# Channel stage: sums' products behind a convolution, attention-out seven ahead, first and last operations shared out differently

## What is computed

```
x = x + attn(cond(x, itok), ...)                    # ends in: o @ Wo.T + bo
# second block, along time (T = 512), per channel and batch
mask = arange(T) < length[batch]
y = causal_conv(x * mask, kernel[channel])          # 512 taps, from 64 complex modes
y = (y + x * mask * D[channel]) * mask
w = (q6 - zero_point) * scale                       # 512 x 512
x = x + y @ w.T + bias
```

## Time and profile before

| | |
|---|---|
| median of 3 runs | 736.43 us (736.04 to 737.22) |
| the profiled execution's own time | 739.18 us |
| its span, first to last instruction | 737.3 us |
| PE busy in the span | 707.4 us (96%) |
| DVE, ACT, POOL busy | 589.8, 412.7, 205.9 us (80%, 56%, 28%) |
| last stage, 572.5 us to the end | 164.8 us |

### The profile page before, as it was taken

The page is one execution under the profiler, slowest core; times in us unless marked ns, Lnnn a source line. Parts: engine busy times, 40 slices in busy tenths (PEclk is TensorE's granted clock), DMA queues, the critical chain, the costliest instruction groups (busy, mean ns, idle before and its releaser), DMA issues.

```text
span 737.3 us, 17037 instructions
## 1 busy us (share of the span) xinstructions
PE 707.4 (96%) x7152; PEld 568.3 (77%) x7152; DVE 589.8 (80%) x1010; ACT 412.7 (56%) x736; POOL 205.9 (28%) x237
## 2 busy tenths in 40 slices
PE   8999999999999999999999999999989799999997
PEld 7767787786978788787869787887667687777785
DVE  5778989998997877697767868777987688788754
ACT  5576565655656765846555565648554444444433
POOL 5361020030002010540300000006200176766676
PEclk9999999999999999999999999999999999999999
DMA  7800100010002001000100010012112678888732
GB/s 224 316 3 2 58 5 1 2 62 2 2 1 63 2 2 58 2 4 13 61 2 2 1 59 2 1 32 74 44 63 49 180 196 207 196 210 182 181 99 101
DMA packets 31919, 50.94 MB, mean 69 GB/s; under 512 B 6594, under 2 KB 21090, under 8 KB 30562
## 3 DMA queue, kind: packets, MB, share of 16 engines
q1 hardware_dynamic: 29858, 49.26, 24.4%
q0 software_dynamic: 1024, 0.53, 0.3%
q10 hardware_dynamic: 960, 0.06, 0.1%
HBM read 41.19 MB, written 8.63 MB: 68 GB/s over the span
## 4 chain that ended last, share of the span: by engine, by line
PE 85%; DVE 8%; ACT 2%; issue 2%; DMA 1%; POOL 1%; SPq 0%; POOLq 0%
PE ps L719 34%; PE ps L611 7%; PE ps L768 7%; PE ps L612 7%; PE ps L613 6%; PE ps L790 5%; PE ps L660 3%; PE ps L1012 3%; PE ps L1017 3%; PE ps L619 2%; PE ps L621 2%; PE ps L620 2%; DVE sum_low L1666 2%; PE ps L988 1%; DVE z_low L1393 1%
## 5 line engine op out<-in xcount | busy, mean ns | idle before, releaser
L1112 ACT ACTIVATE qt<-ps,m_bias 128x512 f32<-128x512 f32 x228 | 145.9, 686 | 88.9 <-PE ps L719 79.6
L719 PE MATMUL ps<-q_high,m_high 64*128 64x512 f32 x768 | 166.6, 398 | 0.6 <-issue 0.3
L719 PE MATMUL ps<-q_high,m_low 64*128 64x512 f32 x768 | 162.3, 388 | 0.0
L719 PE MATMUL ps<-q_low,m_high 64*128 64x512 f32 x768 | 114.2, 387 | 0.0
L719 PEld LDWEIGHTS ps<-q_high,m_high 64*128 64x128 f32 x768 | 89.7, 185 | 16.2 <-issue 6.5
L719 PEld LDWEIGHTS ps<-q_high,m_low 64*128 64x128 f32 x768 | 89.7, 185 | 9.6 <-issue 0.6
L1393 DVE TENSOR_TENSOR z_low<-ps,z_high 128x512 fp32r<-128x512 f32 x128 | 79.7, 681 | 17.8 <-ACT z_high L1132 16.4
L719 PEld LDWEIGHTS ps<-q_low,m_high 64*128 64x128 f32 x768 | 81.5, 184 | 10.0
L1132 ACT CAST z_high<-ps 128x512 fp32r<-128x512 f32 x128 | 66.7, 597 | 13.7 <-PE ps L790 9.2
L1117 ACT ACTIVATE sc<-sc 128x512 f32<-128x512 f32 x60 | 38.1, 635 | 41.5 <-DVE sc L1378 35.9
L600 POOL TENSOR_TENSOR y_low<-y,y_high 128x512 fp32r<-128x512 f32 x32 | 46.8, 1461 | 41.3 <-ACT y_high L1322 41.3
(11 more groups left out here) (251 smaller groups left out, 1470.5 us busy)
## 6 DMA issues: line engine op xcount, KB each, us to landing
x_raw<-in_x_groups SPq DMA_DIRECT2D x32, 256.0 KB
x_t<-in_x_channels SPq DMA_DIRECT2D x8, 1024.0 KB, 8.2
out<-rest SPq DMA_DIRECT2D x32, 256.0 KB, 5.1
toep_high<-taps_scratch SPq DMA_DIRECT2D x32, 192.0 KB, 4.2
toep_low<-taps_scratch SPq DMA_DIRECT2D x32, 192.0 KB, 4.7
w_raw<-in_w_groups SPq DMA_DIRECT2D x8, 512.0 KB, 7.2
toep_far<-taps_scratch SPq DMA_DIRECT2D x32, 64.0 KB, 5.1
rope_raw<-in_rope_rows SPq DMA_DIRECT2D x8, 192.0 KB, 7.3
```

The source lines that it names most:

```text
L719: mm = pe.matmul(ps[:, fold_bank(u, j) + e, :], weights[rows, (GH * g + j) // 2, c, :], moving[c][rows, :], start=start, stop=stop)
L1112: act.activation(qt[:, j, :], ps[:, fold_bank(u, j) + j % 2, :], ACT.Identity, bias=m_bias[:, h:h + 1]).then_inc(s["qt_done"], 1)
```

## The change

- **PE's order.** In iteration c the convolution of channel c comes first, then (at c % 4 = 1) `total`, the layer's product, and last the attention-out of tile c+7. Seven attention-outs (`FIRST_A`) run ahead of the first convolution, where five did.
- **Splits.** From group 2 on they stand at c % 4 = 0 on ACT (behind `sum_high`) and on DVE (ahead of y). `split(1)` is the first thing ACT does in the stage, and its subtraction is POOL's.
- **First low parts.** Those of tiles 0 and 1 are POOL's, in front of its loop; 2 and 3 stay DVE's.
- **Last tiles.** The output tiles 29, 30 and 31 (`BY_DVE_LAST`) get x1 plus bias on ACT, out of order, at c = 32; the last total is computed a second time into bank 0, and DVE adds it times its scale in three operations at c = 34. POOL has no part in them. `through_ffn` is cut in a high and a low half; at the end the high half of tile 29 goes ahead of the low half of tile 28.
- **Setup.** Six small DVE operations at the kernel's start use one step counter instead of two semaphores. ACT waits on that counter before the 6-bit words are turned into floats.

```
@@ -305,8 +305,12 @@
     LAST_SBANK = (BX, BZ, BX, BT + 1)
     LAST = NU - 1
     AHEAD = 5
-    a_bank = lambda i: (0, 1, 2, 3, 7)[i] if i < AHEAD else (i - AHEAD) % 2
+    a_bank = lambda i: (0, 1, 2, 3, 7)[i] if i < 5 else (i - 5) % 2
     BUSY = 2
+    KIND_STEPS = 6
+    FIRST_A = 7
+    BY_DVE_LAST = (C - 3, C - 2, C - 1)
+    LATE_TOTAL_BANK = 0
     s_bank = lambda u, n: (FIRST_SBANK if u == 0 else SBANK)[n]
     BY_DVE = (GH - 3, GH - 1)
     qt_count = lambda u, j: GH * u + j - 2 * max(0, min(u, LAST) - 1) - (sum(h < j for h in BY_DVE) if 1 <= u < LAST else 0)
...
@@ -586,7 +590,13 @@
             pool.tensor_tensor(o_low[0][:, :, 0:EARLY], o_sum[:, 0:4, 0:EARLY], f(o_high[0][:, :, 0:EARLY]),
                                ALU.subtract).then_inc(s["ol_early"], 1)
 
-            for c in range(C + 5):
+            pool.wait_ge(s["oh_done"], 2)
+            pool.tensor_tensor(o_low[1][:], o_sum[:, 4:8, :], f(o_high[1][:]), ALU.subtract).then_inc(s["ol_done"], 1)
+            for i in range(2):
+                pool.wait_ge(s["x1_high_done"], i + 1)
+                pool.tensor_tensor(x1_low[0][:, i], x_t[0][:, i], f(x1_high[0][:, i]), ALU.subtract).then_inc(s["x1_low_done"], 1)
+
+            for c in range(C + 2):
                 i = c - 5
                 if i >= 0:
                     g, n = i // 4, i % 4
...
@@ -967,8 +977,8 @@
                     pe.wait_ge(s["woT_done"], 1)
                     pe.wait_ge(s["zl_done"], 8 * NU)
                     pe.wait_ge(s["s_taken"], 4 * NU)
-                if i >= AHEAD:
-                    pe.wait_ge(s["x1_done"], i - 1 if i >= AHEAD + 2 else i - AHEAD + 1)
+                if i >= 5:
+                    pe.wait_ge(s["x1_done"], i - 1 if i >= 7 else i - 4)
                 part = slice(tt * P, (tt + 1) * P)
                 three(ps[:, a_bank(i), :], woT_high[:, part], woT_low[:, part], run_of(o_high[g % 2][:]),
                       run_of(o_low[g % 2][:])).then_inc(s["a_ready"], 1)
...
@@ -998,7 +1008,7 @@
                 pe.matmul(ps[:, TOTAL_BANK, :], ones_r[:], run_of(sum_high[:]), start=True, stop=False)
                 pe.matmul(ps[:, TOTAL_BANK, :], ones_r[:], run_of(sum_low[:]), start=False, stop=True).then_inc(s["total_ready"], 1)
 
-            def through_ffn(g, n):
+            def ffn_high(g, n):
                 i = 4 * g + n
                 if n == 0:
                     pe.wait_ge(s["yh_done"], 4 * g + 4)
@@ -1011,6 +1021,9 @@
                 for k in range(TT):
                     pe.matmul(ps[:, F_BANK[i % 3], :], wfT[:, k, n * P:(n + 1) * P], run_of(y_high[g % 2][:, k]), start=(k == 0),
                               stop=False)
+
+            def ffn_low(g, n):
+                i = 4 * g + n
                 if n == 0:
                     pe.wait_ge(s["yl_done"], 4 * g + 4)
                 for k in range(TT):
@@ -1018,21 +1031,30 @@
                                    stop=(k == TT - 1))
                 mm.then_inc(s["f_ready"], 1)
 
-            for i in range(AHEAD):
+            for i in range(FIRST_A):
                 attention_out(i // 4, i % 4)
             for c in range(C):
                 g, ch = c // 4, c % 4
-                if c + AHEAD < C:
-                    attention_out((c + AHEAD) // 4, (c + AHEAD) % 4)
-                if g >= 1 and ch == 1:
-                    total(g - 1)
                 convolved(c)
                 if g >= 1:
-                    through_ffn(g - 1, ch)
-            through_ffn(NG - 1, 0)
+                    if ch == 1:
+                        total(g - 1)
+                    ffn_high(g - 1, ch)
+                    ffn_low(g - 1, ch)
+                if c + FIRST_A < C:
+                    attention_out((c + FIRST_A) // 4, (c + FIRST_A) % 4)
+            ffn_high(NG - 1, 0)
+            ffn_high(NG - 1, 1)
+            ffn_low(NG - 1, 0)
             total(NG - 1)
-            for n in range(1, 4):
-                through_ffn(NG - 1, n)
+            for part in (sum_high, sum_low):
+                mm = pe.matmul(ps[:, LATE_TOTAL_BANK, :], ones_r[:], run_of(part[:]), start=(part is sum_high),
+                               stop=(part is sum_low))
+            mm.then_inc(s["total_ready"], 1)
+            ffn_low(NG - 1, 1)
+            for n in range(2, 4):
+                ffn_high(NG - 1, n)
+                ffn_low(NG - 1, n)
 
         @block.scalar
         def _(act):
...
@@ -1149,7 +1171,7 @@
 
             def ffn_float(k):
                 act.wait_ge(s["bits_taken"], k + 1)
-                act.wait_ge(s["kind_step"], 5)
+                act.wait_ge(s["step"], KIND_STEPS)
                 act.activation(q_float[:, k, :], qw[:, k, :], ACT.Identity, scale=unit_of[:, 0:1]).then_inc(s["wf_ready"], 1)
 
             def wo_high():
@@ -1293,26 +1315,33 @@
                     act.wait_ge(s["conv_ready"], 4 * (g - 1))
                 act.copy(x1_high[g % 2][:, tt], x_t[g % RX][:, tt]).then_inc(s["x1_high_done"], 1)
 
-            for i in range(TT):
+            def rest_slot(i):
+                if i >= RW:
+                    act.wait_ge(stored[i % RW], 16 * (i // RW))
+
+            split(1)
+            for i in range(AHEAD):
                 x1_rounded(i)
-            split(1)
-            x1_rounded(TT)
-            for c in range(C + 5):
+            for c in range(C + 2):
                 g, ch, i = c // 4, c % 4, c - 5
                 if ch == 0 and 1 <= g <= NG:
                     act.wait_ge(s["y_summed"], 4 * g)
                     if g >= 2:
                         act.wait_ge(s["total_ready"], g - 1)
                     act.copy(sum_high[:], y_sum[:]).then_inc(s["sum_high_done"], 1)
-                if ch == 1 and 2 <= g + 2 < NG:
+                if ch == 0 and 2 <= g + 2 < NG:
                     split(g + 2)
                 if i >= 0:
                     act.wait_ge(s["total_ready"], i // 4 + 1)
                     act.wait_ge(s["z_scaled"], 1)
-                    if i >= RW:
-                        act.wait_ge(stored[i % RW], 16 * (i // RW))
+                    rest_slot(i)
                     act.activation(run_of(rest[i % RW][:]), ps[:, TOTAL_BANK, :], ACT.Identity, bias=fb_c[:, i % 4:i % 4 + 1],
                                    scale=z_scale[:, i % 4:i % 4 + 1]).then_inc(s["rest_begun"], 1)
+                if c == C:
+                    for j in BY_DVE_LAST:
+                        rest_slot(j)
+                        act.activation(run_of(rest[j % RW][:]), run_of(x_t[(NG - 1) % RX][:, j % 4]), ACT.Identity,
+                                       bias=fb_c[:, j % 4:j % 4 + 1]).then_inc(s["last_begun"], 1)
                 if c + AHEAD < C:
                     x1_rounded(c + AHEAD)
                 if c < C:
...
@@ -1441,17 +1470,12 @@
...
-            dve.tensor_tensor(row_in_block[:], l_pos, block_row[:], ALU.subtract).then_inc(s["row_step"], 1)
-            dve.wait_ge(s["row_step"], 1)
-            dve.tensor_copy(row_kind[:], l_pos).then_inc(s["kind_step"], 1)
-            dve.wait_ge(s["kind_step"], 1)
-            dve.tensor_scalar(row_kind[:], row_kind[:], 3, None, ALU.bitwise_and).then_inc(s["kind_step"], 1)
-            dve.wait_ge(s["kind_step"], 2)
-            dve.tensor_scalar(unit_of[:], row_kind[:], 1.0, None, ALU.is_equal).then_inc(s["kind_step"], 1)
-            dve.wait_ge(s["kind_step"], 3)
-            dve.tensor_scalar(bits_of[:], unit_of[:], 4032.0 - 63.0, 63.0, ALU.mult, ALU.add).then_inc(s["kind_step"], 1)
-            dve.wait_ge(s["kind_step"], 4)
-            dve.tensor_scalar(unit_of[:], unit_of[:], 1.0 / 64.0 - 1.0, 1.0, ALU.mult, ALU.add).then_inc(s["kind_step"], 1)
+            chain(dve.tensor_tensor(row_in_block[:], l_pos, block_row[:], ALU.subtract))
+            chain(dve.tensor_copy(row_kind[:], l_pos))
+            chain(dve.tensor_scalar(row_kind[:], row_kind[:], 3, None, ALU.bitwise_and))
+            chain(dve.tensor_scalar(unit_of[:], row_kind[:], 1.0, None, ALU.is_equal))
+            chain(dve.tensor_scalar(bits_of[:], unit_of[:], 4032.0 - 63.0, 63.0, ALU.mult, ALU.add))
+            chain(dve.tensor_scalar(unit_of[:], unit_of[:], 1.0 / 64.0 - 1.0, 1.0, ALU.mult, ALU.add))
...
@@ -1632,23 +1656,34 @@
 
             for i in range(TT):
                 x1_made(i)
-            for i in range(TT):
+            for i in range(2, TT):
                 x1_rest(i)
-            split(1)
             x1_made(TT)
+            dve.wait_ge(s["x1_low_done"], TT)
             x1_rest(TT)
             dve.wait_ge(s["mask_ready"], TT)
             for c in range(C + 6):
                 g, ch, i = c // 4, c % 4, c - 6
+                if c == C + 2:
+                    dve.wait_ge(s["total_ready"], NG + 1)
+                    dve.wait_ge(s["z_scaled"], 1)
+                    for n, j in enumerate(BY_DVE_LAST):
+                        dve.wait_ge(s["last_begun"], n + 1)
+                        dve.scalar_tensor_tensor(out=run_of(rest[j % RW][:]), in0=ps[:, LATE_TOTAL_BANK, :],
```

(15 more changed lines are left out.)

## The result

| | before | changed |
|---|---|---|
| median, us | 736.83 (4 runs) | 727.83 (4 runs, 726.97 to 729.96) |
| span of the profiled execution | 737.3 | 728.1 |
| the channel stage, first attention-out to last output | 161.04 | 152.02 |

The ratio is 0.9883, 95% interval 0.9861 to 0.9904, so the change gives 7 to 10 us; 8.15 was forecast. The stage is what the changed kernel touches.

What follows compares the result with a forecast made beforehand. PE was taken as back to back except waits for sum_low (7.8 us) and o_low (4.9). Start 3.45 + totals 5.05 - end 0.35 = 8.15, from 736.43 to 728.3; own range 726 to 730.5, overall 724.0 to 733.4.

Steps and rivals of the forecast that it cites:

- start: Stage up to the first layer's product: 3.45 us gained, bounds 1.85 to 4.5.
- totals: PE's waits for sum_low before totals in the channel loop: 5.05 us gained, bounds 1.5 to 8.7.
- end: Last tiles: product 31 waits for output 28, 0.35 us lost; bounds 0.45 earlier to 0.9 later.
- The idle 0.4: At the start PE stops at 576.2 and goes on at 576.6, instead of idling 3.85 us.
- the clock at 1.00: Granted clock at 2.4 GHz throughout; if idle stretches cost it again, the start gives 1.85 instead of 3.45 us.
- x1 of tile 8 late: Group 2's x lands at 587, x1 of tile 8 wants it about 590; 1 us late if DMA took 12.
- the waits' order: PE's waits before totals: short at c = 5 and 9, some 0.8 at 13, 17, 21, none at 25, 29.
- Nothing by itself in the loop: Seven attention-outs ahead instead of five gain nothing in the loop, as no wait for x1 stands there.
- it fills 1.4 us of the start: Seven attention-outs ahead instead of five fill 1.4 us of the start, counted in the start's 3.45.
- (a): Rival: the totals' waits go whole, delay not carried round the group; 12.25 us gained, 724.2; chance 0.2.
- (b): Rival: the wait moves with the total and the clock falls at the start; 3.0 us gained, 733.4; chance 0.18.
- (c): Rival: slower than before, DVE becomes the bound of the loop; 738.5; chance 0.04.

Runs made afterwards that it cites:

- its seed: Changed kernel with ACT's copy of split(g+2) ahead of sum_high instead of behind it; median 725.78 us, ratio 0.9838 to the kernel before.
- its carrier: Changed kernel without POOL's addition of x1 to output tiles 0 to 28; median 724.01 us, ratio 0.9816 to the kernel before.
- The other order at the end: Changed kernel, ACT's split ahead of sum_high, one early ACT operation behind rest tile 28, one late-total DVE addition behind output 28; 724.60 us, ratio 0.9824.
- the start alone: Kernel before with split(1) first on ACT, its subtraction and two low parts on POOL, PE's order untouched; 735.30 us, ratio 0.9963.
- total and start: Kernel before with total behind the convolution, split(1) first on ACT, its subtraction and two low parts on POOL; 725.61 us, ratio 0.9834.
- the start alone once more: Same program as the start alone, no edit, executed again; stage 158.32 us, execution 737.13 us.
- six ahead twice: Changed kernel with FIRST_A = 6 instead of 7; 728.26 us, ratio 0.9877, stage 152.27; executed again unedited, stage 152.24.
- the total alone: Kernel before with only total moved behind the convolution of channel 4g+1; 729.49 us against 738.31, ratio 0.9879.
- the stretch filled: The start alone plus six unused PE products ahead of the first convolution; 734.67 us, ratio 0.9955 to the kernel before.

## Why the prediction was right

The forecast was 728.3, the measured median is 727.83. The terms, each from starts in the two traces; the border between the first two is the first layer's product:

| term | forecast | measured | how |
|---|---|---|---|
| start | 3.45 | 3.36 | first layer's product 20.29 after the first attention-out (593.42 - 573.13) against 22.96, 2.67; one attention-out more done, 0.69 |
| totals | 5.05 | 5.90 | from there to the layer's product behind the last convolution: 125.77 before, 119.18 after, less the 0.69 |
| end | -0.35 | -0.24 | from there to the last output: 12.31 and 12.55 |
| stage | 8.15 | 9.02 | |

**Start.** The idle 0.4 is 0.20; the first convolution was put 6.8 after the first attention-out and came 6.75 after; the wait before it (1.3 forecast, 1.15), the wait of attention-out 7 for x1 (0.8 forecast, 0.71) and the clock at 1.00 came as laid out. DVE's two low parts and POOL's two took their turns, as the rule of the Trainium skill has it ("SBUF — State Buffer", section "Who interferes with whom"): 2.85 us for DVE's two and 2.99 for POOL's, where four on DVE take 2.48 and POOL's subtraction 1.29 when nothing is in the way. The experiment with all four on DVE shows that sharing them cost 0.45 instead of saving anything. "x1 of tile 8 late" did not happen. That the clock stays up was a bound, not a certainty: at 1.8 us idle it fell in two of the profiled executions and stayed in three; the changed kernel's 1.15 is shorter.

**Totals.** The mechanism was right step by step: DVE idle for o_high behind `sum_high`, y late, `y_pair` and x1's low part blocked by POOL two channels later, the last `y_sum` late (0.55 forecast, 0.46 by 648.23 against the convolution's 648.79, where it was 1.02 ahead before), nothing lost at c = 25 and 29. Both experiments that cut the chain, at its seed and at its carrier, give 2.6 to 2.85 and cycles of 17.81 to 17.83. Sizes were off: the loss in the steady cycle is 0.62 (18.44 - 17.82), I had 0.9; `sum_low` comes 4.63 after the convolution of channel 4g, I had 4.8. At c = 9 I had 0.55, since I let the first group start with little delay; it is 0.91 (616.60 - 597.87 - 17.82), more than in the steady cycle; the split at c = 8 waits for o_high as long as the later ones do (1.46), and what makes the difference is not followed here. At c = 5 it is 0.1 instead of 0.4 (597.87 - 593.42 = 4.45 against 4.34 of work). So the waits' order was wrong, too: 0.53 at c = 9 and 0.36 at 13, 17 and 21, where a short one and then some 0.8 were expected. The errors at 9 and at the others go opposite ways; in sum 0.85 too little gain. One reading was incomplete: the earlier trace rows starts at 500 us, and PE also waits 2.8 us there for `sc_last`, at 543.13, ahead of the stage; that wait is the same in both kernels.

**End.** PE's product 31 waits for output 28, as said, and the end lost 0.24. The wait is 0.53 by the profile, forecast 0.9: DVE reached output 28 0.2 earlier than laid out, and by the distance of starts PE lost some 0.7. (ACT's three operations took 1.94, not about 1.7, but the chain did not go through them.) POOL is out of the last three tiles, but not out of the chain: DVE's output 27 waits 1.36 for POOL's addition, and behind it stand the three late additions and output 28. Without that addition the end is 0.73 shorter. The other order at the end takes 0.63 off.

**Seven ahead.** "Nothing by itself in the loop" holds, but "it fills 1.4 us of the start" does not: the kernel before had six ahead, not five, and with six the changed kernel's stage is only 0.22 to 0.25 longer.

**Rivals.** (a), all waits gone, is not what this order does, but it is what the swap on ACT makes of it. (b) and (c) did not occur. What I had not asked is whether the split had to move: in the loop the total's move alone gives 8.84, and the change as a whole 5.90.

## What to carry to other kernels

When a wait stands at one product, first try moving that product alone behind work that is ready; here that alone gives 8.0 us of the stage, 8.8 in the loop, and the whole change 9.0. Before putting an operation ahead of a critical one on its engine, follow what it waits for on the other engine's queue: a copy that was ready long ago stood behind one that waits for the group's last sum, and a swap of two lines gives 2.85 us back. DVE operations with both inputs in SBUF and POOL operations beside them are best laid out as one queue (`sum_low` takes 0.68 alone and 1.77 beside `y_low`); a delay that makes them meet in another phase can be carried round a loop, even though every engine has idle time on average.

## What was unexpected

After an idle stretch of 1.80 to 1.82 us of PE, the granted clock fell to half in two profiled executions (the start alone, and total and start) and stayed at full in three (the start alone once more, six ahead twice). The same program did both. After 3.85 us it fell in both kernels that have it (before, and the total alone), but not for equally long: in the second it cost 0.8 us more at the start, with no edit there. So stages of single executions differ by about 1 us through the clock alone, and a part's worth is better read from the stretch that it touches. A fall after 1.8 us costs about 1 us: the stage of the start-alone kernel was 159.49 with it, 158.32 without it and 158.50 with the stretch filled. What decides between the executions is open; no run here tells.

Two low parts on POOL beside two on DVE took DVE 2.85 us, four on DVE alone 2.48 us: a shared-out operation that meets such blocking was slower than one engine doing it all.
